# Layer one's attention weight as a squared sigmoid of a logarithm, in batches of twelve units

## The reference

```
q2 = sum(Q*Q); k2 = sum(K*K)
sq = q2 + k2.T - 2 * Q @ K.T
dist = sqrt(max(sq, 0))
W = (1e-4 + dist) ** -2
W = W / (1e-4 + sum(W, axis=-1))
A = W @ V                 # for each of 2 x 16 heads
s = xn + (G * A) @ W_out.T + b_out
```

## Time and profile before

| | us |
|---|---|
| median of 3 runs | 6949.82 (6949.76 to 6949.85) |
| profiled execution, its own time | 6951.07 |
| its span, first to last instruction | 6949.3 |
| busy in the span: VectorE | 6639.4 (96%) |
| ScalarE | 6429.0 (93%) |
| TensorE, matmuls | 3988.7 (57%) |
| GpSimd | 3429.4 (49%) |

### The profile page before, as it was taken

One profiled execution on the slowest core, in us unless ns is written; L12 is line 12 of the kernel. 1 busy time (PEld: TensorE's weight loads), 2 busy tenths in 40 slices (PEclk: granted clock), 3 DMA queues, 4 the chain that ended last, 5 costly groups with the idle time before them and its releaser, 6 DMA issues. The chain is left out here.

```text
span 6949.3 us, 55640 instructions
## 1 busy us (share of the span) xinstructions
PE 3988.7 (57%) x17072; PEld 1356.5 (20%) x17072; DVE 6639.4 (96%) x6316; ACT 6429.0 (93%) x3748; POOL 3429.4 (49%) x1422
## 2 busy tenths in 40 slices
PE   5777767777677776454454454454454444454555
PEld 3222222222222242011111111121111111111112
DVE  7899999999999967999999999999999999999997
ACT  3699999999999934999999999999999999999997
POOL 0244444444444400656556565565656556565654
PEclk8888888898988887565666556565665665566557
DMA  3100000000000032000000000000000000000003
GB/s 130 56 14 14 16 12 16 12 16 11 16 11 16 7 138 85 6 15 8 9 15 9 8 15 9 8 15 9 11 12 9 8 15 9 8 15 9 15 6 99
DMA packets 238999, 157.45 MB, mean 23 GB/s; under 512 B 148998, under 2 KB 222617, under 8 KB 237418
## 3 DMA queue, kind: packets, MB, share of 16 engines
q1 hardware_dynamic: 238826, 155.32, 8.0%
HBM read 95.74 MB, written 59.51 MB: 22 GB/s over the span
## 5 line engine op out<-in xcount | busy, mean ns | idle before, releaser
L1306 POOL TENSOR_TENSOR work<-work 128x1776 f32<-128x1776 f32 (+3 forms) x696 | 2149.0, 3088 | 55.3
L1098 PE MATMUL psS<-q_stack,k_stack 96*128 96x512 bf16 x2048 | 1034.6, 608 | 1757.4 <-DVE work L1214 1691.5
L750 POOL TENSOR_SCALAR work<-work 128x2048 f32<-128x2048 f32 x512 | 970.6, 1896 | 1218.8 <-DVE work L952 1199.4
L940 DVE SCALAR_TENSOR_TENSOR work<-work,psS 128x1024 f32<-128x1024 f32 x1024 | 1217.2, 1213 | 44.7 <-ACT work L899 44.5
L1303 POOL TENSOR_SCALAR work<-work 128x1776 f32<-128x1776 f32 (+2 forms) x174 | 290.8, 1671 | 1953.2 <-ACT work L1188 1945.9
L1209 DVE TENSOR_SCALAR work<-psS 128x1024 f32<-128x1024 f32 x1024 | 1204.7, 1218 | 41.5 <-PE psS L1098 17.2
L1214 DVE TENSOR_TENSOR work<-psS,work 128x1024 f32<-128x1024 f32 x1024 | 1200.3, 1213 | 0.0
L899 ACT ACTIVATE work<-psS 128x1024 f32<-128x1024 f32 x1024 | 1152.2, 1125 | 50.1 <-PE psS L768 49.5
L1220 DVE SCALAR_TENSOR_TENSOR work<-work 128x2048 f32<-128x2048 f32 x512 | 1139.0, 2283 | 30.1 <-ACT work L1184 30.1
L768 PE MATMUL psS<-q_stack,k_stack 102*128 102x512 bf16 x2048 | 709.8, 433 | 654.4 <-DVE work L940 620.5
L914 ACT ACTIVATE work<-work 128x2048 f32<-128x2048 f32 x512 | 1032.2, 2016 | 2.4 <-POOL work L750 2.4
(11 more groups left out here) (140 smaller groups left out, 3812.6 us busy)
## 6 DMA issues: line engine op xcount, KB each, us to landing
qk_parts<-work SPq DMA_DIRECT2D x64, 384.0 KB, 3.2
q_stack<-qk_parts SPq DMA_DIRECT2D x384, 64.0 KB, 2.3
k_stack<-qk_parts SPq DMA_DIRECT2D x384, 64.0 KB, 2.3
xT_store<-work SPq DMA_DIRECT2D x2, 4096.0 KB, 16.5
ffn_in<-xT_store SPq DMA_DIRECT2D x64, 128.0 KB, 2.5
work<-in_x SPq DMA_DIRECT2D x1, 4096.0 KB, 14.2
xn_store<-work SPq DMA_DIRECT2D x1, 4096.0 KB, 13.0
work<-xn_store SPq DMA_DIRECT2D x4, 1024.0 KB, 11.7
```

The costliest lines, as they stand in the source:

```text
L750: nc.gpsimd.tensor_scalar(slot, slot, F32_MAX, 0.0, ALU.min, ALU.max).then_inc(s_m, 1)
L940: nc.vector.scalar_tensor_tensor(part, part, 0.5 / SHEP_EPS, m.psS[half][:, :], ALU.add, ALU.mult).then_inc(s_y, 1)
L1098: last = nc.tensor.matmul(m.psS[half][:, q * 512:(q + 1) * 512], m.k_stack[b][0:ROWS, kt * P:(kt + 1) * P], m.q_stack[b][0:ROWS, c:c + 512 ...
L1306: nc.gpsimd.tensor_tensor(part, part, part, ALU.mult).then_inc(s_pp, 1)
```

## The change

```diff
@@ projection_phase, sync
-                if L == 1:
-                    sp.wait_ge(s_vfree, 4 * i + 6)
-                    sp.dma_start(io["v_store"][:, bass.ds(4 * i, 4), :], m.values[:, bass.ds(4 * i, 4), :])\
+                sp.wait_ge(s_vfree, 4 * i + 6)
+                sp.dma_start(io["v_store"][:, bass.ds(4 * i, 4), :], m.values[:, bass.ds(4 * i, 4), :])\
+                    .then_inc(s_vst, 16)
+                if L == 0:
+                    sp.dma_start(io["g_store"][:, bass.ds(4 * i, 4), :], m.gated[:, bass.ds(4 * i, 4), :])\
                         .then_inc(s_vst, 16)
@@ distance_phase
-    RING = 8
-    LAG_PV = 6
-    LAG_INV, LAG_SQ = 3, 4
-    ACT_SQ = 416
+    BATCH = 12
+    LANES = 18
+    LAG_PV = 16
+    AHEAD = 4
+    POOL_SQ = 1152
+    sizes = [4] + [BATCH] * ((TOTAL - 8) // BATCH) + [4]
+    starts = [sum(sizes[:j]) for j in range(len(sizes) + 1)]
@@ distance_phase, sync, for each tile n
+                if n >= B:
+                    sp.wait_ge(s_pv, KT * (n - 1))
+                sp.dma_start(m.v_tile[b][:, :, 0:DH], views["v_store"][:, b, :, h, :]).then_inc(s_vt[b], 16)
...
+                if n >= 2:
+                    store_out(n - 2)
+                sp.dma_start(gate[:, n % 2, :].rearrange("p (t d) -> p t d", d=DH), views["g_store"][:, b, :, h, :])\
+                    .then_inc(s_gate[n % 2], 16)
+                if n >= 1:
+                    store_ffn(n - 1)
@@ distance_phase, tensor
+            def scores(g):
...
+                for half in range(2):
+                    if g > 0:
+                        pe.wait_ge(s_gd, 2 * (g - 1) + half + 1)
...
+            def weighted(g):
...
+                pe.wait_ge(s_wd, g // 2 + 1)
+                pe.wait_ge(s_wp, g // 2 + 1)
...
+            HIDDEN = {6: 0, 7: 1, 8: 2, 9: 3}
+            SUM = {13: (0, 1), 14: (2, 3, 4), 15: (5, 6, 7)}
+            for g in range(TOTAL + KT + 4):
+                n, kt = g // KT, g % KT
+                if g < TOTAL:
+                    scores(g)
+                if 0 <= g - LAG_PV < TOTAL:
+                    weighted(g - LAG_PV)
...
@@ distance_phase, scalar
+            for i in range(NB):
+                for g in range(starts[i], starts[i + 1], 2):
+                    act.wait_ge(s_gd, 2 * (g + 2))
+                    nc.scalar.activation(lane(g, 2), lane(g, 2), ACT.Ln, scale=1.0 / (SHEP_EPS * SHEP_EPS))\
+                        .then_inc(s_ln, 2)
+                nc.scalar.preload_act_table_set("sigmoid_and_others")
+                for g in range(starts[i], starts[i + 1], 2):
+                    act.wait_ge(s_ln, g + 2)
+                    nc.scalar.activation(lane(g, 2), lane(g, 2), ACT.Sigmoid, scale=-0.5).then_inc(s_sg, 2)
...
@@ distance_phase, vector
+            def guard(g):
+                if g >= LANES:
+                    dve.wait_ge(s_pv, g - LANES + 1)
+                for half in range(2):
+                    dve.wait_ge(s_qk, 2 * g + half + 1)
+                    nc.vector.tensor_scalar(lane(g)[:, 0, half * 1024:(half + 1) * 1024], m.psS[half][:, :], ZERO_SHIFT,
+                                            None, ALU.max).then_inc(s_gd, 1)
+            def squares(g):
+                dve.wait_ge(s_sg, g + 2)
+                part = lane(g, 2)[:, :, POOL_SQ:T]
+                nc.vector.tensor_tensor(part, part, part, ALU.mult).then_inc(s_wd, 1)
...
+            def beside(g):
+                n, kt = g // KT, g % KT
+                if kt == 0 and 1 <= n <= TILES:
+                    ffn_out(n - 1)
+                if kt == 1 and n >= 2:
+                    out_copy(n - 2)
+                if kt == 5 and n >= 2:
+                    head_out(n - 2)
+                if n < TILES and kt in (8, 10):
+                    relu(n, (kt - 8) // 2)
+                if n < TILES and kt in (9, 11):
+                    relu_squared(n, (kt - 9) // 2)
...
+            guards(0, starts[1] + 1)
+            for i in range(NB):
+                done = starts[i + 1] + 1
+                for p, g in enumerate(range(starts[i], starts[i + 1], 2)):
+                    squares(g)
+                    if 1 <= p <= AHEAD:
+                        guards(done, done + 1)
+                        done += 1
+                if i + 1 < NB:
+                    guards(done, starts[i + 2] + 1)
@@ distance_phase, gpsimd
+            for g in range(0, TOTAL, 2):
+                pool.wait_ge(s_sg, g + 2)
+                part = lane(g, 2)[:, :, 0:POOL_SQ]
+                nc.gpsimd.tensor_tensor(part, part, part, ALU.mult).then_inc(s_wp, 1)
@@ output_phase, sync
+                if L == 0 or c >= 2:
+                    sp.dma_start(o_sb[:, t, :], io["o_store"][:, t, :]).then_inc(s_ol[c], 16)
+                if L == 0 or c == CH - 1:
+                    sp.dma_start(g_sb[:, t, :], io["y_store"].rearrange("t p d -> p t d")[:, t, :]).then_inc(s_yl[c], 16)
                 if L == 0:
                     sp.dma_start(xn_sb[:, t, :], io["xn_store"][:, t, :]).then_inc(s_al[c], 16)
                     sp.dma_start(x_sb[:, t, :], x_view[:, t, :]).then_inc(s_xl[c], 16)
```

More of the change, by code:

```diff
@@ L693, in distance_phase @@
     loads = 2 * len(PRODUCTS) + 2
[L694 to L701 removed]
+    ring = m.area(0, LANES, T)
@@ L758, in pe_scores @@
-        def pe_scores(pe, h, u, first, halves=(0, 1)):
-            b, kt = u // KT, u % KT
-            if kt == 0 and halves[0] == 0:
-                pe.wait_ge(s_stk[b], 16 * loads * (h + 1))
-            for half in halves:
-                if not (first and u == 0):
-                    pe.wait_ge(s_y, 2 * (UNITS * h + u) + half - 1)
-                for q in range(2):
-                    c = (2 * half + q) * 512
-                    last = nc.tensor.matmul(m.psS[half][:, q * 512:(q + 1) * 512],
-                                            m.k_stack[b][0:rows, kt * P:(kt + 1) * P],
-                                            m.q_stack[b][0:rows, c:c + 512], start=True, stop=True)
-                last.then_inc(s_qk, 1)
@@ L773, in pe_values @@
-        def pe_values(pe, h, u, first):
-            n = UNITS * h + u
-            b, kt = (u % UNITS) // KT, u % KT
-            if kt == 0:
-                pe.wait_ge(s_vt, 2 * h + (u // KT) + 1)
-                if not (first and 0 <= u < UNITS):
-                    pe.wait_ge(s_o, 2 * h + (u // KT) - 1)
-            pe.wait_ge(s_wa, n + 1)
-            pe.wait_ge(s_wd, n + 1)
-            for q in range(QB):
-                last = nc.tensor.matmul(m.psO[b][VW * q:VW * (q + 1), :], m.v_tile[b][:, kt, :],
-                                        ring[:, u % RING, q * 512:(q + 1) * 512], start=kt == 0, stop=kt == KT - 1)
-            last.then_inc(s_pv, 1)
@@ L801, in pe_hidden @@
                 if quarter == 0:
                     pe.wait_ge(s_fin, 16 * (n + 1))
-                g = HALVES[quarter // 2]
-                for f in range(2 * (quarter % 2), 2 * (quarter % 2) + 2):
+                    if n >= 1:
+                        pe.wait_ge(s_r2, 2 * n - 1)
+                    if n >= 2:
+                        pe.wait_ge(s_g, n - 1)
+                if quarter == 2 and n > 0:
+                    pe.wait_ge(s_yo, n)
+                first = 2 * (quarter % 2)
+                for f in range(first, first + 2):
@@ new lines, in ffn_hidden, with ffn_sum @@
+                                                m.ffn_in[:, k, :], start=k == 0, stop=k == KD - 1)
+                if first:
+                    last.then_inc(s_h, 1)
+            def ffn_sum(n, fs):
+                if fs[0] == 0:
+                    pe.wait_ge(s_r2, 2 * (n + 1))
+                for f in fs:
+                    last = nc.tensor.matmul(m.psM[0][:, 0:D], m.hidden[:, f, :], m.w2T[:, f, :], start=f == 0,
+                                            stop=f == FT - 1)
+                if fs[-1] == FT - 1:
+                    last.then_inc(s_yps, 1)
@@ L965, in _ @@
-            pairs(dve, head)
+            def guard(g):
[9 more added lines that the diff above has]
+                nc.vector.tensor_tensor(part, part, part, ALU.mult).then_inc(s_wd, 1)
@@ new lines, in guards @@
+            def guards(first, last):
+                for g in range(first, min(last, TOTAL)):
+                    guard(g)
+                    beside(g)
+            guards(0, starts[1] + 1)
[8 more added lines that the diff above has]
+                    guards(done, starts[i + 2] + 1)
@@ L968, in out_homes, with _ @@
+            for g in range(TOTAL, TOTAL + KT + 6):
+                beside(g)
+        @block.gpsimd
+        def _(pool):
+            for g in range(0, TOTAL, 2):
+                pool.wait_ge(s_sg, g + 2)
+                part = lane(g, 2)[:, :, 0:POOL_SQ]
+                nc.gpsimd.tensor_tensor(part, part, part, ALU.mult).then_inc(s_wp, 1)
 def out_homes(m):
```

351 lines of the change are left out of this document (140 added, 211 removed).

## The result

| | us |
|---|---|
| kernel before, median of 4 runs beside it | 6949.84 (6949.76 to 6951.31) |
| changed kernel, median of 4 runs | 7377.49 (7377.01 to 7382.64) |
| ratio, with its 95% interval | 1.0616 (1.0598 to 1.0635) |
| span of the changed kernel's profiled execution | 7376.2 |

The change costs 6.2%. The forecast was 7380, and the 426.9 us by which the span grew (7376.2 - 6949.3) divide much as it divided them: 413.7 of them in layer one's attention, 14.9 between that stage's last division and layer two's first pass.

What follows compares the result with a forecast made beforehand. GpSimd and VectorE excluding each other and a ring of waits make a batch 60.8 us; the attention stage grows 417 to 2615, other stages add 15: 432 on 6951.07, forecast 7380 us, range 7250 to 7560.

Steps and rivals of the forecast that it cites:

- Exclusion: Sigmoid phase, layer one's attention: GpSimd's and VectorE's squares alternate, each waiting for the whole other, 5.77 us a pair of units.
- the engine totals: Attention batch of 12 units: ScalarE's work 44.8 us, VectorE's 42.6; by these alone the change would save 286 us.
- The table switch: ScalarE between logarithms and sigmoids: 1.3 us a switch, two a batch, not the skill page's 2.66.
- The division's multiply: VectorE's last division step meets GpSimd in some 5 of 16 positions, waiting up to 3.9 us: 1.2 a batch.
- The run of guards: After a batch's squares, VectorE's seven guards at 2.27 us, 15.9 in all, plus interspersed work and TensorE delays, before the last logarithm.
- Rival (d): TensorE's clock stays low through every run of guards: 7.3 us more a batch, 7690 us; chance 0.07.
- The first race: Each batch's first square: VectorE assumed ahead of GpSimd; the opposite order adds 164 us, giving 7545, chance 0.17.
- Ends: Attention stage outside 41 batches of 60.8 us: about 60 before the first full batch's first sigmoid, 62 for the last batch.
- The signs: Expected in the new profile: long alternating squares, ScalarE idle 12 to 15 us a batch, batches 61 us apart, ScalarE about 75% busy.
- The rest: Outside the attention stage: output stage + 10 us, last head's store + 3, projection stores + 2, per-tile transfers 0; 15 in all.

Runs made afterwards that it cites:

- pool_small: The changed kernel with GpSimd squaring only 2 x 64 of its 2 x 1152 columns, the others left unsquared: 7015.0 us.
- act_share2: The changed kernel with VectorE's 896 columns of each square squared on ScalarE instead, GpSimd's 1152 kept: 7109.6 us.
- small_ahead3: The changed kernel with GpSimd squaring only 2 x 64 columns and two more VectorE guards ahead of each batch's squares: 6767.0 us.
- pool_all: The changed kernel with all squares on GpSimd and none on VectorE, whole computation done: 6726.4 us.
- pool_first3: The changed kernel with eight small memsets on VectorE ahead of each batch's first square, to let GpSimd go first: 7538.5 us.
- pool_first: The changed kernel with one 64-column memset on VectorE ahead of each batch's first square, to let GpSimd go first: 7380.8 us.
- ahead2: The changed kernel with two more guards on VectorE's list ahead of each batch's squares: 7156.1 us.
- ffn_light2: The changed kernel with most of layer one's FFN matmuls left out from the second row tile on: 7342.3 us.

## Why the prediction was right, step by step

**Exclusion.** The pair step of 5.77 us was read from two short instructions at the other end of the program and held: 5.77 and 5.76 in the timeline, the sixth square ending 34.5 us after the first sigmoid's start (1555.92 + 3.58 - 1525.00) where the sum had 34.3. So it is in 32 of the 42 batches. pool_small prices the exclusion at 362 us, act_share2 shows that it needs both engines, and small_ahead3 and pool_all bring the batch down to 46.0 and 44.9 us, where the engine totals had promised 44.8. By those totals alone the change would have saved 286 us; in pool_all it does save 223 (6949.8 - 6726.4), with the stage's ends and the longer output stage in that number.

The Trainium skill ("SBUF — State Buffer", "Who interferes with whom") says that a VectorE instruction with two SBUF inputs and a GpSimd instruction that reads SBUF exclude each other for the whole instruction; all these runs agree. The 0.115 us from release to start that its section "A bandwidth-pool intuition that's wrong" gives, for DMA descriptors held up by VectorE, would have added 58 us; it isn't seen in the steps of 5.77, and the sum was right to do without it.

**The table switch.** 1.31 us from the end of a logarithm to the start of the sigmoid, where the earlier trace rows had 1.32: the load starts at 1584.68, 0.01 after the last logarithm's 1581.05 + 3.62, and the first sigmoid at 1585.98. The 2.66 us of the Trainium skill ("ScalarE: Activation LUTs", "What ACT_TABLE_LOAD costs") would, with two switches beside two times 21.17 us of passes, have made 47.7 us of the batch in pool_all; it is 44.93.

**The division's multiply.** The prediction gave 1.2 us a batch to it, for a wait of up to 3.9 in 5 of 16 positions. The size was about right, the way there was another. The multiply itself waits little: it takes 893 ns in the mean where it took 0.42 us, 15 us in all, 0.36 a batch. But in every fourth batch, ten in all, it stands between VectorE's second and third square, and takes the turn that the square would have had:

```profile
1718.29 1.15 DVE L904 TENSOR_TENSOR work<-work,den 128x256 f32<-128x256 f32 x1
1719.36 5.84 DVE L879 TENSOR_TENSOR work<-work 128x1792 f32<-128x1792 f32 x1
1725.13 2.34 DVE L873 TENSOR_SCALAR work<-psS 128x1024 f32<-128x1024 f32 x2
```

GpSimd's next multiply starts 0.24 us before the third square, which then waits for all of it. In these ten batches the sixth square ends 38.7 us after the first sigmoid's start, 4.17 later than in the other 32: 1.0 us a batch, and the 63.5 us of every fourth batch. In pool_small, where GpSimd has little to do, the multiply takes 426 ns and no batch shows this step; that moving the division would win the 1.0 us back is not shown, since no run moved it.

**The run of guards.** From the end of the last square to the release of the last logarithm the sum had 20.4 us (seven guards at 2.27, and 2.2, 0.6 and 1.7 for what lies among them) beside that 1.2. The mean over 41 batches is 20.2, from 19.4 to 22.1; the batch shown, whose division falls into this run, has 1581.05 - 1559.50 = 21.5. TensorE and its clock were put at 0.6 + 1.7 = 2.3 us and VectorE waited 122.9 / 42 = 2.9 for scores, in this batch most where FFN matmuls stand between. That the clock would come up within the run was right. Windows of one batch:

```profile
1557.00:1561.00 4.00, 2.27 (x10) 0.33 (x10) 4.00 (x3) 0.00 (x0) 4.00 (x2) 0.50 0.00 0
1561.00:1565.00 4.00, 3.90 (x13) 0.68 (x12) 3.68 (x7) 3.14 (x1) 2.39 (x1) 0.50 0.09 11
1565.00:1569.00 4.00, 4.00 (x27) 2.49 (x27) 3.04 (x3) 0.48 (x1) 0.00 (x0) 0.90 0.85 137
1569.00:1573.00 4.00, 4.00 (x27) 1.85 (x25) 3.41 (x5) 3.62 (x1) 0.00 (x0) 1.00 0.55 136
```

TensorE is at 0.50 (1.2 GHz) until 1565, rises within the next stretch (0.90) and is at 1.00 (2.4 GHz) in the last one; in the 4 us before 1565 it was busy for 3.90. Rival (d), a low clock through every run, would have had score matmuls of 1.03 for two; their median is 389 ns, and only their mean is 449. The prediction's price for (d) has a gap: its 3.7 us a guard is worked out nowhere, and its own 0.86 for each of the five guards not yet at the lower level makes 4.3 us a batch, about 7560 instead of 7690.

**The first race.** The prediction let VectorE win it and gave the other outcome 17% and 7545 us. Both times hold, the second as pool_first3 shows (7538.5). But the outcome hung on about 0.1 us, which nothing in the trace of before could tell; here the forecast was lucky rather than reasoned.

**Ends.** The first full batch's sigmoids start 62.6 us into the stage (forecast 60), 41 batches of 60.62 follow (60.8), and 63.0 for the last (62). In this last stretch TensorE waits 20.83 us for a copy of a finished head that stands in VectorE's list behind the last four squares, and then does 96 weighted-sum matmuls, 12.19 us, in one piece. That copy's place wasn't in my sum, whose 62 covered it by chance.

**The signs.** Of the signs named, GpSimd's squares (5.75 us), the distance of the batches, ScalarE's share (74%) and the score matmul's median came as said. Two fell just outside: VectorE's squares have a mean of 3.42 us instead of 3.5 or more, and ScalarE's wait for guards is 653.9 / 42 = 15.6 us a batch instead of 12 to 15.

**The rest.** From the stage's last division to layer two's first pass it is now 2929.50 - 2860.75 = 68.8 us; before, to the row here, 2501.55 - 2447.68 = 53.9:

```profile
2501.55 1.91 ACT L296 ACTIVATE work<-work 128x2048 f32<-128x2048 f32 x1 [8.99 <-PEq L124]
```

That is 14.9 more, where I had 10 + 3. SP's first load starts 6.5 us after the division instead of 2.35, since it waits for the last head's store, and the first product is added 15.4 us after that load instead of 8.4. The projection stage's 16 stores cost nothing (the attention starts 0.7 earlier than before, not 2 later), nor do the transfers per tile: ahead of the division's first multiply, which waits for the gate, VectorE's idle time is 0.2 us in all, ahead of the weighted sums TensorE's is 0.0. Everything else in the program moved by 1 us.

**Where the loss comes from**, then: two engines that exclude each other were given the same step at the same moment, 362 us, and the order of VectorE's list makes it wait for the sigmoid and ScalarE for the guards behind the squares, another 221 to 248 us; without either the change would gain some 183 (6767 against 6950, in a kernel that leaves part of the squares out) or, by pool_all, which leaves nothing out, 223.

## What to carry to other kernels

Before a step is split between two engines, look whether the two can work in SBUF at the same time: a split that looks balanced by totals costs the sum of both parts, and it also blocks the faster engine for everything else in its list. Even a short instruction with two operands in SBUF, placed between the squares, cost a whole turn here (4.17 us for the division's multiply). Where two engines wait for each other in turn once per batch, count the ring from one start to the next, not the engines' totals, and fill the pause before the first result with work of the next batch. When the order of two instructions that exclude each other is decided by one shared release, fix it by a wait or by moving one of them away (the wait was not tried; act_share2 and pool_all move VectorE's squares away), since some 0.05 us decided over 2%.

## What the hardware showed that was not expected

**The order is settled a little behind GpSimd's recorded start.** A square of VectorE that came 0.03 us after the start of GpSimd's multiply still went first, in 43 of the 44 batches of pool_first; one that came 0.08 us after it waited for all of GpSimd's 3.9 us, in 43 of the 44 of pool_first3. In ahead2 the same happened to the squares that came some 1.07 us late, in nine batches. The Trainium skill ("SBUF — State Buffer", "Who interferes with whom") says that issue order decides who blocks; the runs agree, but for the squares of pool_first, which by the recorded starts came second.

**GpSimd's rate.** In place, 2304 columns took 4027 ns and 4096 took 7027, 1.67 ns a column for what is added, without VectorE in the way.

**Taking matmuls away makes the others longer.** In ffn_light2 the score matmul's mean rose from 449 to 476 ns and the granted clock over the whole span fell from 0.681 to 0.659.
